# A Mamba–FFN–attention–MoE kernel: softplus in two VectorE steps, roots by Ln and Exp, and part of the front moved into the scan phase

## The reference, cut to what matters

```python
xn = layer_norm(x)                              # per token, 256 channels; four chunks of 64 channels
for each chunk c of 4:                          # mamba, D_INNER 128, D_STATE 16
    xi, z = split(in_proj(xn_c)); xc = silu(conv4(xi)); dt, Bs, Cs = split(x_proj(xc))
    dt = softplus(dt_proj(dt) + b)
    h  = exp(dt * A) * h + (dt * xc) * Bs       # scan over 1024 tokens, for each of 16 states
    y  = (sum_s h * Cs + xc * D) * silu(z);  ym_c = out_proj(y) + skip * xn_c
x1 = x + proj(layer_norm(ym))
x2 = x1 + fp8 ffn(layer_norm(x1)) + bias        # quantized operands, one 256x256 product
g  = group_norm(layer_norm(x2))                 # 32 groups
x3 = x2 + wp @ softmax(Q K^T / 16) V + bp       # channel attention, scores are 256x256
out = x3 + moe(layer_norm(x3))                  # 8 experts, top 2, hidden 1024
```

## Time and profile before

| | us |
|---|---|
| median of 3 runs | 1981.06 |
| the profiled execution | 1983.14 |
| its span | 1981.2 |
| start, to the first scan | 102.88 |
| scan phase, each of 4 | 213 to 214 |
| between, each of 3 (end of gate L1369 to first scan) | 116 to 119 |
| last between, without a next batch | 93 |
| mixture of experts | 579 |

### The profile page before, as it was taken

How to read it: one execution, slowest core, us unless ns; L and a number is a source line. 1 busy time by engine, 2 the same in 40 slices (tenths; PEclk the granted TensorE clock), 3 DMA queues, 4 the chain that set the end, 5 groups by cost and what they waited for, 6 DMA issues and landing times. The chain is left out here.

```text
span 1981.2 us, 20702 instructions
## 1 busy us (share of the span) xinstructions
PE 1528.7 (77%) x5773; PEld 941.8 (48%) x5806; DVE 1346.4 (68%) x1441; ACT 767.4 (39%) x1201; POOL 1166.9 (59%) x605
## 2 busy tenths in 40 slices
PE   5467678867677886777786677767369999999997
PEld 2122224542222453222444222235258888888887
DVE  2899998579999768999867899983642222222222
ACT  6535334654442664444277353322112222222222
POOL 0699892359987038989513998930045554545543
PEclk9689999979999997999998899988579999999999
DMA  3075560146554015646202655653102222222222
GB/s 117 27 270 198 189 204 23 41 166 215 193 180 139 23 61 202 211 163 214 84 22 83 243 202 181 207 219 137 66 24 41 33 40 35 38 37 37 37 33 27
DMA packets 80697, 230.71 MB, mean 116 GB/s; under 512 B 12844, under 2 KB 31605, under 8 KB 77270
## 3 DMA queue, kind: packets, MB, share of 16 engines
q1 hardware_dynamic: 64694, 210.93, 30.6%
q0 software_dynamic: 15904, 18.66, 5.9%
HBM read 208.15 MB, written 19.82 MB: 115 GB/s over the span
## 5 line engine op out<-in xcount | busy, mean ns | idle before, releaser
L390 PE MATMUL psum<-HC_sb,ident_sb 128*128 128x512 f32 x1024 | 493.7, 606 | 65.1 <-DVE HC_sb L1362 57.4
L390 PE MATMUL psum<-experts_sb 64*128 64x512 f32 (+5 forms) x930 | 307.7, 562 | 240.6 <-DVE HC_sb L1362 149.3
L952 ACT ACTIVATE psum<-experts_sb 128x1024 f32<-128x1024 f32 x256 | 285.5, 1117 | 506.8 <-DVE experts_sb L1352 393.8
L1352 DVE TENSOR_TENSOR_SCAN experts_sb<-psum,DBX_sb 128x1024 f32<-128x1024 f32 x172 | 389.7, 2275 | 31.7 <-POOL DBX_sb L1042 30.7
L390 PEld LDWEIGHTS psum<-HC_sb,ident_sb 128*128 128x128 f32 x1024 | 190.0, 192 | 282.0 <-issue 131.8
L390 PEld LDWEIGHTS psum<-experts_sb 64*128 64x128 f32 (+5 forms) x962 | 97.9, 153 | 473.9 <-DVE HC_sb L1362 240.7
L1886 DVE TENSOR_TENSOR YS_sb<-psum_moe,b_sb 128x256 f32<-128x256 f32 x71 | 30.1, 424 | 353.5 <-PE psum_moe L1641 349.9
L1734 ACT ACTIVATE hgt_sb<-psum_moe,b_sb 128x256 f32<-128x256 f32 (+1 forms) x312 | 116.5, 456 | 381.2 <-PE psum_moe L1641 381.2
L1641 PE MATMUL psum_moe<-XGT_sb,w1s_sb 128*128 128x256 f32 (+1 forms) x1248 | 253.6, 362 | 0.0
L1641 PE MATMUL psum_moe<-experts_sb,hgt_sb 128*128 x1136 | 251.7, 379 | 0.7 <-DVE YS_sb L1886 0.7
L1618 POOL DMA_INDIRECT out<-YS_sb,scat_sb x71 | 131.7, 1855 | 203.9 <-DVE YS_sb L1890 188.7
(11 more groups left out here) (264 smaller groups left out, 1742.7 us busy)
## 6 DMA issues: line engine op xcount, KB each, us to landing
DA_sb<-bc_rows SPq DMA_DIRECT2D x128, 512.0 KB, 4.6
experts_sb<-bc_rows SPq DMA_DIRECT2D x64, 512.0 KB, 3.7
SQ_sb<-bc_rows SPq DMA_DIRECT2D x64, 512.0 KB, 4.2
X_XT_sb<-bc_rows SPq DMA_DIRECT2D x64, 512.0 KB, 5.5
experts_sb<-w1T SPq DMA_DIRECT2D x8, 1024.0 KB, 19.3
experts_sb<-w2T SPq DMA_DIRECT2D x8, 1024.0 KB, 21.3
X_sb<-x_tok SPq DMA_DIRECT2D x5, 1024.0 KB, 7.1
experts_sb<-x_tok SPq DMA_DIRECT2D x4, 1024.0 KB, 4.8
```

Of the source, the lines that this page charges most:

```text
L390: return nc.tensor.matmul(o, lhsT, rhs, start=start, stop=stop, **k)
L952: nc.scalar.activation(decays[i % 2], DT[:, c, :], ACT.Exp, scale=a_neg[:, s:s + 1]).then_inc(da_ready, 1)
L1352: v.tensor_tensor_scan(STATE[i % STATE_SLOTS], decays[i % 2], DRIVE[i % STATE_SLOTS], 0.0, ALU.mult, ALU.add).then_inc(h_ready, 1)
```

## The change

It rearranges the front; `build_moe` stays as it is. The parts, with the names of the code:

1. `log1p`: two VectorE steps a chunk in place of five. ScalarE takes a scaled and shifted Ln, a Square and a Relu (one pass more a chunk). The `exp_ln` of before is split in `exp_of` and `logs_of`.
2. Roots: the group norm's and the last token norm's reciprocal roots come from Ln and Exp(-0.5·) on ScalarE with three or four small VectorE steps that refine them. The FFN input norm's scale goes into its Sqrt.
3. Last norm: the router logits are made from unnormed x3. Its mean is folded into `gate_w`, and `route` multiplies by the reciprocal root. The norm itself, for the tokens that are stored, moves into iterations 4 to 7 of the next batch's scans on ScalarE; after the last batch it stays behind `tm_copy`.
4. POOL: dt of chunks 2 and 3 moves into the scan phase (behind drive 2 and drive 8); dt of chunk 0 is held until `group_scale` is done, dt of chunk 1 until `weigh` is; `add_ffn_bias` goes, its bias comes from one more bf16 matmul a tile in `ffn`. `f_nb` of the first norm moves from VectorE to POOL.
5. z: `z_pair` stands behind `gate` on TensorE, and `silu_z` behind the first two decays on ScalarE. B/C products stand behind dt of chunk 3.
6. SyncE: three B rows are loaded ahead of the spread; `store_tm`, `load_next` and `load_x` stand at iterations 8, 10 and 13 of the scan phase.
7. POOL_READS is (2, 6, 10, 14); the last chunk is gated, projected and skipped in halves, and `y_turn` follows in `scans`.
8. First and second norm of x1, x2: each half is normed as soon as its factors are there.

```diff
-POOL_READS = (3, 7, 11, 15)
+POOL_READS = (2, 6, 10, 14)
-SP_STEPS = 5
+SP_STEPS = 2
...
             for i in range(NI):
                 load_b(0, i)
-                if i == POOL_READS[0]:
+                load_c(0, i)
+                if i == NEXT_AT:
                     sp.wait_ge(xh_turned, CT)
                     load_next(1)
-                load_c(0, i)
+                if i == X_AT:
+                    sp.wait_ge(dt_done, NC)
+                    load_x(0)
             with sp.Fori(1, B) as b:
-                sp.wait_ge(x1_done, b * NB)
-                load_x(b)
                 store_bc(b)
-                load_b(b, 0)
-                load_b(b, 1)
+                for i in range(3):
+                    load_b(b, i)
                 spread_bc(b)
                 store_x3(b - 1)
-                store_tm(b - 1)
                 sp.wait_ge(gate_done, b)
+                sp.sem_inc(tokens_there, 1)
                 for i in range(2, NI):
-                    load_b(b, i)
-                    if i == POOL_READS[0]:
+                    if i >= 3:
+                        load_b(b, i)
+                    if i == TOKENS_AT:
+                        store_tm(b - 1)
+                    if i == NEXT_AT:
                         sp.wait_ge(stored, b * 32)
+                        sp.sem_inc(tokens_there, 1)
+                    load_c(b, i)
+                    if i == NEXT_AT:
                         load_next(b + 1)
-                    load_c(b, i)
+                    if i == X_AT:
+                        sp.wait_ge(dt_done, b * NC + NC)
+                        sp.sem_inc(tokens_there, 1)
+                        load_x(b)
...
     # TensorE, between(p, b)
                 gram(p)
                 hc_turn(p, 0)
+                if go_on:
+                    dt_linear(b, 2)
                 group_var(p)
-                if go_on:
-                    bc_linear(b)
                 hc_turn(p, 1)
                 scores(p)
                 if go_on:
-                    dt_linear(b, 2)
                     dt_linear(b, 3)
+                    bc_linear(b)
                 attend(p)
-                if go_on:
-                    z_pair(b, 0)
                 out_linear(p)
-                if go_on:
-                    z_pair(b, 1)
                 tm_turn(p, 0)
                 tm_turn(p, 1)
                 gate(p)
+                if go_on:
+                    z_pair(b, 0)
+                    z_pair(b, 1)
                 pe.wait_ge(gate_done, p + 1)
...
     # ScalarE, between(p, b), from the second copy of the turned tokens
+                scores(p)
+                if go_on:
+                    logs_of(b, 1)
+                    read_dt(b, 2)
+                softmax(p)
+                if go_on:
+                    read_dt(b, 3)
+                attend(p)
                 if go_on:
                     read_bc(b)
-                scores(p)
-                if go_on:
-                    exp_ln(b, 1)
-                softmax(p)
-                if go_on:
-                    read_dt(b, 2)
-                attend(p)
-                if go_on:
-                    read_dt(b, 3)
-                    exp_ln(b, 2)
-                    exp_ln(b, 3)
-                    silu_z(b, 0)
-                nc.scalar.preload_act_table_set(SQRT)
-                token_sqrt(3, p, eps5)
-                token_norm(3, p, TM, X2, tm_done)
+                    for c in range(2, NC):
+                        exp_of(b, c)
+                        logs_of(b, c)
                 tm_copy(p, 0)
+                token_rsqrt(p)
                 tm_copy(p, 1)
-                if go_on:
-                    silu_z(b, 1)
+                if not go_on:
+                    last_norm(p, range(NB))
...
     # ScalarE, scans(b, after)
                 for i in range(NI):
                     decay(i)
+                    if i == 1 and after:
+                        silu_z(b, 0)
+                        silu_z(b, 1)
+                        nc.scalar.preload_act_table_set(EXP_LN)
+                    if 4 <= i < 8 and after:
+                        last_norm(b - 1, (2 * i - 8, 2 * i - 7))
...
     # POOL
+            def between(b):
+                pool.wait_ge(g_step, b * 5)
+                steps_of_dt(b, 0)
+                pool.wait_ge(att_done, b * 2)
+                steps_of_dt(b, 1)
+                split_bc(b)
+
+            def first_shift(b):
+                pool.wait_ge(f_small, b * 2 + 1)
+                nc.gpsimd.tensor_tensor(f_nb[:, :], f_neg[:, :], f_rs[:, :], ALU.mult).then_inc(f_small, 1)
...
                 for i in range(NI):
                     drive(i)
+                    if i == STATE_SLOTS - 1:
+                        steps_of_dt(b, 2)
+                    if i == 8:
+                        steps_of_dt(b, 3)
+                    if i == FIRST_AT + 2 * NB + NB // 2 + 1:
+                        first_shift(b + 1)
...
     # VectorE
+            def log1p(b, c):
+                n = b * NC + c
+                t, log = square_tile(c), log_tile(c)
+                dve.wait_ge(sp_sq, n + 1)
+                v.scalar_tensor_tensor(t, t, SERIES_REST, DT[:, c, :], ALU.add, ALU.mult).then_inc(sp_step, 1)
+                dve.wait_ge(sp_step, n * SP_STEPS + 1)
+                dve.wait_ge(sp_ln, n + 1)
+                v.scalar_tensor_tensor(log, t, SERIES_TOP, log, ALU.min, ALU.add).then_inc(sp_step, 1)
...
     # VectorE, between(p, b)
                 group_scale(p)
                 softmax(p)
                 weigh(p)
                 if go_on:
+                    log1p(b, 1)
                 out_weight(p)
                 x3(p)
                 if go_on:
+                    log1p(b, 2)
+                last_rstd(p)
+                route(p)
+                if go_on:
                     log1p(b, 3)
-                route(p)
...
-                gate(NC - 1)
-                skip(NC - 1)
+                last_chunk()
```

More of the change, by code:

```diff
@@ L1 @@
+import math
 from collections import namedtuple
@@ L341, in _ @@
                 sp.dma_start(dst, src).then_inc(w_rest, 16)
-            load_x(0)
             for name, _ in ROUTING_CONSTANTS:
@@ L710, in scans @@
                 xhat_turn(b + 1, 1)
+                y_turn(b)
             pe.wait_ge(w_first, W_FIRST)
@@ L828, in hc_copy, with group_rsqrt @@
                 nc.scalar.activation(halves(HCC[:, c, :]), psum[:, 2:4, :], ACT.Copy).then_inc(hcc_done, 1)
-            def group_sqrt(p):
+            def group_rsqrt(p):
                 act.wait_ge(g_var_ready, p + 1)
-                nc.scalar.activation(g_std, psum[:, 0, 0:2], ACT.Sqrt, bias=eps5[:, :]).then_inc(g_std_ready, 1)
+                nc.scalar.activation(g_log, psum[:, 0, 0:2], ACT.Ln, bias=eps5[:, :]).then_inc(log_done, 1)
+                act.wait_ge(log_done, p * 3 + 1)
+                nc.scalar.activation(g_rs, g_log, ACT.Exp, scale=-0.5).then_inc(g_std_ready, 1)
             def scores(p):
@@ L1064, in _ @@
             with pool.Fori(1, B) as b:
-                between(b - 1, b)
+                between(b)
                 scans(b, True)
-            between(B - 1, None)
         @block.vector
@@ L1413, in _ @@
             round_weights(ffn_w[:, :, :], SQ[:, 0, 0:CT * C].rearrange("p (c o) -> p c o", c=CT), ffn_q[:, :, :])
-            fold(v.tensor_copy(FBB, FB[:, :]))
-            fold(v.tensor_copy(FB[:, :], FBB))
+            prep(v.tensor_tensor(scal[:, 6:7], scal[:, 1:2], scal[:, 1:2], ALU.mult))
+            prep(v.tensor_scalar(scal[:, 7:8], scal[:, 6:7], 1e-5, None, ALU.mult))
+            prep(v.reciprocal(scal[:, 8:9], scal[:, 5:6]))
+            prep(v.memset(ones_b[:, :], 1.0))
+            prep(v.memset(FB_PARTS[:, :], 0.0))
+            fold(v.tensor_copy(FBB, FB))
+            fold(v.tensor_scalar(FB, FBB, scal[:, 8:9], None, ALU.mult))
+            for k in range(3):
+                fold(v.tensor_copy(FBB, FB))
+                fold(v.tensor_copy(FB_PARTS[32 * k:32 * k + 1, :], FBB[32 * k:32 * k + 1, :]))
+                if k < 2:
+                    fold(v.tensor_tensor(FB, FB, FBB, ALU.subtract))
             for c in range(CT):
```

305 lines of the change are left out of this document (165 added, 140 removed).

## The result

The changed kernel takes 1920.62 us (median of 4 runs, 1918.70 to 1922.75); the kernel before took 1979.76 beside it. The ratio is 0.9698, 95% interval 0.9678 to 0.9718: 3.0% faster. The forecast was 1918, with a range from 1898 to 1950.

The account below looks back on a forecast made before the run. VectorE bounds the scan phases, a chain hopping between engines the stretches between. Start and batch 0 -9.4, three batches -50.4, last -5.3: together -65 us from the profiled 1983.1, giving 1918 us, range 1898 to 1950.

Parts of the forecast that it names:

- End of the phase, -2.4: End of each scan phase: earlier last product (about 1.6 us) and halved last chunk (about 0.8) start y_turn 2.4 us earlier.
- Logits, gate matmuls end at 403.8: Between batches: raw tokens turned directly behind out_linear, so gate matmuls start at 397.0 and end at 403.8, 17 us earlier.
- Route at 404, sz_done at 410.9, first product at 415.3: Between batches: route ahead of log1p(3), then z gates, then first product at 415.3 instead of 436.23, 20.9 us earlier, three times.
- Rival 2: Between batches: the port keeps route late, three VectorE steps each waiting up to 2.1 us for POOL; +19, 1937; chance 0.14.
- dt(2) and dt(3), 7.3 us in batch 0 and 2.0 later: Scan phase: POOL's added dt pairs delay scans 3, 5 and 9 in batch 0, only scan 9 (2.0 us) later.
- f_nb on POOL, +1.6: Scan phase, iteration 34: POOL loses its lead, drives 36 and 37 come late; 1.6 us net, four times.
- DMA, 0: Scan phase, SyncE's queue: B row 11 lands before it is wanted; taken as 0, unknown from 0 to 8 us a batch.
- rival 4: Iterations 8 to 13: SyncE's queue holds B rows back and starves POOL; +78, 1996 us; chance 0.05.
- rival 5: Between batches: z gates behind route hold the scans as long as dt did; about 1978 us, no change; chance 0.04.
- rival 1: Scan phase: POOL becomes the bound and doesn't recover, each phase paying 11.6 us; +27, 1945 us; chance 0.16.
- Rival 3: Better: dt(3) hides wholly and the longer stretches 2 and 3 give back their extra 2.5 us; 1903; chance 0.11.
- Last stretch, -5.3: After the last scans: gains of 2.4, 1.8 and about 2.1, less 0.9 for the roots; nothing at the tail.

Follow-up runs that it names:

- experiment 8: Changed kernel with POOL_READS put back from (2, 6, 10, 14) to (3, 7, 11, 15): 1916.05 us, ratio 0.9662.
- Experiment 1: Changed kernel with one added wait: POOL begins its drives of batches 1 to 3 only after last_rstd's small VectorE steps: 1893.09 us, ratio 0.9554.
- experiment 6: Changed kernel with dt(2) and dt(3) back in front of the first drive on POOL: 1910.47 us, ratio 0.9639.
- experiment 9: Changed kernel with the four POOL passes of dt(2) and dt(3) spread over iterations 2, 6, 10 and 14: 1921.05 us, ratio 0.9687.
- experiment 4: Kernel before with one edit alone, f_nb computed on POOL instead of VectorE: 1973.18 us, ratio 0.9952.

## Why the prediction was right, and where its steps were not

The time was right to 2.6 us, and that was luck, because errors cancelled: the stretches between batches came out 14.8 us worse than forecast, the scan phases 10.6 us better, start and last stretch 1.9 better, and 1.5 us had been kept back for the rest. The gain itself, forecast as 65 us, was 59.1 between the medians; the start from the profiled 1983.1, above the median, took up the difference. And one of the prediction's own signs of being wrong came true: the stretches were to be some 20 us shorter (121.5 to 100 from the last gate to the first product), and were 13 to 14 shorter (121.48 to 107.58 from batch 0 to 1).

- **Start, -18.3: right.** Measured -19.0, first scan at 83.88 against a forecast of 84.6.
- **End of the phase, -2.4: too large.** Last product on VectorE: 1.2 us by experiment 8, where 1.6 was taken. And its other side was missing from the sum: the shift by one iteration costs 2.4 to 3.2 us of waits for POOL a phase. In all the edit brought nothing; a loss of up to 7 us is possible.
- **Logits, gate matmuls end at 403.8: too cautious.** That was 86.8 us behind y_turn; measured 81.3 (383.1 - 301.80).
- **Route at 404, sz_done at 410.9, first product at 415.3: too early.** Behind y_turn these are 87.0, 93.9 and 98.3 us; measured 90.1, 98.8 and 103.2. This is the step that failed: 4.9 us in batch 1. Of these, 3.1 are route. The sum has no term for the four steps of last_rstd, with 0.2 us between the gate matmuls and route; measured were 8.8 us (383.1 to 391.9), because POOL held log1p(2) by some 3 us and three of the four steps by 2.0 to 2.1 each. The other 1.8 are ScalarE's waits of 1.24 and 0.56 us for TensorE between the passes of SiLU, which the sum put at nothing; TensorE ran there at a clock of 0.50. Rival 2 had the mechanism of the hold and a chance of 0.14, with its price of 6.3 us a stretch (three steps of 2.1). It looked for it in the 128x2048 additions, which were held 0.15 us (2.44 against 2.29), and in log1p(2), where its sign of over 3 us came true (3.26), but not in 128x8 steps. Experiment 1 shows it: without POOL's passes the four steps take 0.17 us each, and the stretch is 8 to 10 us shorter. The Trainium skill (SBUF — State Buffer, Who interferes with whom) says that a VectorE instruction with two SBUF inputs contends with a POOL instruction that reads SBUF, and that the shared port pair is an exclusive lock. The trace agrees, with 2.2 us for a step of 0.17, and shows it for a tile as small as 128x8; the one-input reciprocal of the same size was not held.
- **dt(2) and dt(3), 7.3 us in batch 0 and 2.0 later: sizes off.** Measured at the places named: 0.69 and 4.22 us in batch 0, and 3.0 us at scan 9 later, with 0.8 to 1.2 more at scan 13. The terms were read from a lead of three drives; experiments 6, 8 and 9 show that the total of POOL's work and the place of its products set the waits as much. The sum also gave VectorE 12.7 us for four iterations by adding durations that overlap; by their starts they take 12.1 (139.33 to 151.45 in the kernel before), so POOL with its 11.6 has little slack to recover in.
- **f_nb on POOL, +1.6: right in its place, wrong in its sum.** The scans behind it waited 0.49 and 1.21 us in batch 0 and 0.53 and 1.21 later. But the row of what it replaced was never read: L1097 took 5.79 us in the phase of the kernel before, where the sum took 0.2. Batch 0 paid 8.4 us of waits, near the forecast of 8.9; less these 5.8 and 1.2 for the end that is the +1.4 of the table. Batches 1 to 3 paid 7 where 3.6 was forecast, and the same row covered it. The parts of this balance are not isolated: in experiment 4 the row alone was worth 3.4 to 3.9 us a phase. This missed row hid most of the error between the batches.
- **DMA, 0: about 1 us too low.** In batches 1 to 3 the drive of iteration 11 waited 2.03, 1.78 and 1.37 us for its B row. From there POOL ran without a gap to drive 13, for which scan 13 waited 1.21, 1.16 and 0.75 us. In batch 0 no drive waited for a B row, and scan 13 did not wait. No run tests it alone. Batch 1:

```profile
434.37 2.35 POOL L1090 TENSOR_TENSOR SQ_sb<-SQ_sb,experts_sb 128x1024 f32<-128x1024 f32 x1 [2.03 <-DMA SQ_sb<-bc_rows]
```
```profile
443.74 2.29 DVE L1401 TENSOR_TENSOR_SCAN experts_sb<-psum,DBX_sb 128x1024 f32<-128x1024 f32 x1 [1.21 <-POOL DBX_sb L1090]
```

- **Rivals 4, 5 and 1 are out.** Waits stand at a few places, and POOL recovers. But the 7 to 8 us that each phase paid lie between the forecast's 3.6 and rival 1's 11.6 (whose terms, 4.9 + 4.9 + 1.6, add up to 11.4). Rival 3 is out too: dt(3) did not hide.
- **Last stretch, -5.3: about right.** Measured -4.1 behind y_turn, where -2.9 was left; a trace can't tell the two apart, since this part differs by 4 us from one execution to another. There no POOL pass is about, and the same steps of last_rstd took 0.17 us:

```profile
1328.94 0.17 DVE L1356 SCALAR_TENSOR_TENSOR token_rs_sb<-token_fix_sb,token_rs_sb 128x8 f32<-128x8 f32 x1
1329.14 0.17 DVE L1358 SCALAR_TENSOR_TENSOR token_nb_sb<-token_mv_sb,token_rs_sb 128x8 f32<-128x8 f32 x1
1333.10 0.22 DVE L1362 TENSOR_TENSOR logits_sb<-psum,token_rs_sb 128x64 f32<-128x64 f32 x1 [3.79 <-PE psum L408]
```

Open: what the halved last chunk is worth by itself (not tried alone), how much of the waits at iterations 9 to 14 is due to late B rows, and how the 28.5 us of experiment 1 divide between the hold and TensorE's clock, which moved together.

## What to carry to other kernels

When an engine is given a head start, ask what it will disturb while it runs ahead: POOL's first drive was done 7 us or more before its scan; the three drives and the dt pair behind them made the path between batches 8 to 10 us longer, and one added wait was worth 1.5%. Read the duration of every small instruction beside the path, not only of the large ones: a mean over a group hides that the same 128x8 step takes 0.17 us in one place and 5.79 in another. A change of many parts that lands on its forecast may still hold parts that lose: here the moved dt passes (12 us by the medians) and perhaps the reads (up to 7 us).

## What the runs showed of the hardware

- A VectorE step of 128x8 with two SBUF inputs takes 0.17 us alone and up to 2.26 us when it starts just behind the start of a POOL pass of 2.35 us. A one-input step of that size took 0.17 us in the middle of such a pass (204.68).
- It can be held for more than one pass: 5.79 us while POOL ran three in a row. What decides is open, since the step at 385.02 got through at 387.2 between two passes that stand as close together (383.86 to 387.18, then from 387.15).
- Such holds work both ways with large steps: POOL's drive took 3.32 us beside log1p(2), 2.35 otherwise, and L1158 took 3.26 us instead of 1.23.
- From the start of TensorE's `direct` to the first product took 4.22 us at a granted clock of 0.57, and 2.45 us at 1.00 (experiment 1).
